# Bias tables moved to GpSimd, an earlier batch load, other drains between GpSimd's sums, and filler products on TensorE

## What is computed

```python
# 1: group norm, 8 heads of 16, two relative-position biases, causal in t
att = einsum('bhqd,bhkd->bhqk', q, k) / sqrt(16) + bias_t + bias_p
x = x + (softmax(where(causal, att, -inf)) @ v) @ Wo
# 2: additive attention on the layer-normed tokens, HID = 16
hidden = tanh(A[:, :, None, :] + B[:, None, :, :])      # 768 x 768 x 16 per batch
t = t + softmax(hidden @ w2 + b2) @ v
# 3: mixture of 8 experts, top 2, capacity 1920, layer norm before
slot = position of the token among those of its expert, over all batches
t = t + sum over 2 experts of weight * (gelu(x w1 + b1) w2 + b2)
```

## Time and profile before

| what | value |
|---|---|
| median of 3 runs | 2385.2 us (2379.06 to 2388.39) |
| the profiled execution | 2384.78 us, of which the trace's span is 2383.0 us |
| mean granted TensorE clock | 0.951 |
| busy share of the span | PE 86%, ACT 71%, DVE 70%, POOL 61% |
| first exponential on ScalarE | 92.63 us |
| first full pass to last full pass | some 122 us a pass |
| pass 14, pass 15, pass 16 start | some 1876, 1977 and 2064 us |
| first expert product | 2124.64 us |

### The profile page before, as it was taken

The page is one execution under the profiler, slowest core; times in us unless marked ns, Lnnn a source line. Parts: engine busy times, 40 slices in busy tenths (PEclk is TensorE's granted clock), DMA queues, the critical chain, the costliest instruction groups (busy, mean ns, idle before and its releaser), DMA issues.

```text
span 2383.0 us, 56242 instructions
## 1 busy us (share of the span) xinstructions
PE 2053.2 (86%) x17665; PEld 1122.5 (47%) x17665; DVE 1675.7 (70%) x4534; ACT 1683.2 (71%) x1933; POOL 1461.3 (61%) x1525
## 2 busy tenths in 40 slices
PE   2889999989998999989998999999999977549986
PEld 1344444444444444444444444444444433338775
DVE  5787787787878787868786878787877665324433
ACT  5238787877887788778787878788878977613332
POOL 3006576656666656565666666666657877627777
PEclk7799999999999999999999999999999988869998
DMA  4546322322222223222323131313131000025553
GB/s 94 89 86 128 95 48 61 55 62 56 61 56 61 56 59 57 58 60 51 66 50 68 42 70 29 81 32 77 32 65 32 12 6 4 7 54 90 84 86 37
DMA packets 157499, 137.99 MB, mean 58 GB/s; under 512 B 24665, under 2 KB 149814, under 8 KB 157104
## 3 DMA queue, kind: packets, MB, share of 16 engines
q1 hardware_dynamic: 119376, 109.87, 22.5%
q0 software_dynamic: 23824, 16.85, 5.2%
q10 hardware_dynamic: 13968, 7.30, 1.2%
HBM read 82.68 MB, written 54.52 MB: 58 GB/s over the span
## 4 chain that ended last, share of the span: by engine, by line
PE 39%; DVE 22%; issue 13%; DVEq 9%; POOL 6%; ACT 4%; POOLq 3%; DMA 2%; SPq 0%; another core or an unknown queue 0%; ACTq 0%
PE logits L978 12%; DVE max_halves L1261 4%; POOL out_dram L583 4%; PE ring L1052 3%; PE av_bank L964 3%; POOLq L802 3%; PE ring L1074 3%; PE ring L1066 3%; PE scores L948 3%; PE scores L951 2%; ACT hidden L902 2%; DVE logit_bias L1447 2%; POOL hidden L803 2%; PE ring L1071 2%; DVEq L1448 2%
## 5 line engine op out<-in xcount | busy, mean ns | idle before, releaser
L803 POOL TENSOR_SCALAR hidden<-b_rep,a_cols 128x768 f32<-128x768 f32 x1152 | 1057.1, 920 | 765.6 <-issue 302.9
L902 ACT ACTIVATE hidden<-hidden 128x2304 f32<-128x2304 f32 x384 | 816.1, 2125 | 16.4 <-POOL hidden L803 16.4
L978 PE MATMUL logits<-hidden,w_shifted 128*32 128x384 f32 x6144 | 591.6, 504 | 65.3 <-ACT hidden L906 30.9
L879 ACT ACTIVATE probs<-scores 128x512 f32<-128x512 f32 (+1 forms) x768 | 391.9, 545 | 325.6 <-PE scores L951 320.9
L1261 DVE TENSOR_REDUCE max_halves<-ring 128x1 f32<-128x384 f32 (+4 forms) x896 | 471.3, 550 | 115.8 <-PE ring L1052 114.2
L906 ACT ACTIVATE hidden<-b_rep,a_cols 128x768 f32<-128x768 f32 x384 | 358.4, 933 | 0.0
L1052 PE MATMUL ring<-k_max,q_max 112*128 112x384 bf16 (+4 forms) x1024 | 296.0, 319 | 34.8 <-DVE max_halves L1261 25.9
L978 PEld LDWEIGHTS logits<-hidden,w_shifted 128*32 128x32 f32 x6144 | 164.0, 110 | 314.9 <-issue 246.7
L948 PE MATMUL scores<-bias_q,onehot_k 112*128 112x512 bf16 (+1 forms) x768 | 276.4, 360 | 4.8 <-ACT probs L879 1.8
L951 PE MATMUL scores<-q_parts,k_parts 98*128 98x256 bf16 (+1 forms) x1536 | 277.3, 262 | 0.0
L814 POOL DMA_INDIRECT expert_rows<-rows,slots x198 | 199.5, 1007 | 64.2 <-issue 32.7
(11 more groups left out here) (262 smaller groups left out, 2585.8 us busy)
## 6 DMA issues: line engine op xcount, KB each, us to landing
qk_parts<-qk_parts_sb SPq DMA_DIRECT2D x16, 1152.0 KB, 4.7
q_parts<-qk_parts SPq DMA_DIRECT2D x192, 96.0 KB, 3.2
k_parts<-qk_parts SPq DMA_DIRECT2D x192, 96.0 KB, 4.3
q_max<-qk_parts SPq DMA_DIRECT2D x96, 96.0 KB
k_max<-qk_parts SPq DMA_DIRECT2D x96, 96.0 KB
expert_rows<-clear_row ACTq DMA_DIRECT2D x9, 792.0 KB, 5.0
x_in<-in_x_dram SPq DMA_DIRECT2D x96, 64.0 KB
x<-in_x_dram SPq DMA_DIRECT2D x96, 64.0 KB
```

Source lines behind the costliest of these rows:

```text
L803: last = g.tensor_scalar(hidden[:, q % SLOTS, o, :], b_rep[:, side], 1.0, a_cols[:, side, a_col(q, o):a_col(q, o) + 1], ALU.mult, ALU.add)
L879: s.activation(probs0[:, d % 3, 2 * pair:2 * pair + 2, 0:n_], scores[:, pair].rearrange("p (j l) -> p j l", j=2)[:, :, 0:n_], ACT.Exp) \
L902: s.activation(hidden[:, t % SLOTS, 0:3, :], hidden[:, t % SLOTS, 0:3, :], ACT.Tanh)
L978: last = mm(logits[32 * g:32 * g + 32, half, 0:HALF], w2_shifted[:, k, :], hidden[:, q % SLOTS, g, HALF * half:HALF * half + HALF], start= ...
```

## The change

- GpSimd, not VectorE, splits the bias table and copies it out to `bias_q[0:64]`, behind its own setup and its first transfer. A new semaphore `bias_made` releases ScalarE's copies (1) and TensorE's first scores (2). Three parts are masked apart and added in two steps.
- SyncE issues `load_x(1)` right after the weight loads, once batch 0 is transposed, and the copies of ScalarE's tables only behind the store of the parts of batch 0. For batch 0 the "k" rest lies in `x2`.
- GpSimd's drains: ahead of each of the three sums at ticks 7 to 18, in all passes; at the other ticks ahead of the third sum only.
- ScalarE: in pass 15 `exp_logits` stands between the two tanh of its tick; at tick 9 of pass 16 a Gelu on one column follows.
- TensorE: `keep_warm(n)` issues n products of 112 x 512 bf16 into the unused `scores` bank, three per tick in pass 15, and 14, 4, 16 and 90 at ticks 3, 7, 8 and 12 of pass 16.

```diff
--- before.py
+++ after.py
@@ -107,6 +107,7 @@
 CLEAR_AT = tuple(range(1, 19, 2))
 CLEARS = 1 + len(CLEAR_AT)
 RING = 3
+WARM_AT = {3: 14, 7: 4, 8: 16, 12: 90}
 PARTS = 4
 
 
@@ -262,7 +263,11 @@
         max_halves = sb("max_halves", [P, H, len(MAX_PARTS)])
         max_parts = sb("max_parts", [4 * TB, 2, 2, P], BF16)
 
-        qk_rest = [xT[:], x_in[:].rearrange("p b c -> p (b c)")]
+        def qk_rest(w, c):
+            if w == 0:
+                return xT[:]
+            return (x_in if positive(c) else x2)[:].rearrange("p b c -> p (b c)")
+
         a_masked = xnT[:, 0:HALF]
 
         q_parts = sb("q_parts", [99, H, L], BF16)
@@ -313,6 +318,7 @@
         setup_pe = sem("setup_pe")
         setup_dve = sem("setup_dve")
         setup_act = sem("setup_act")
+        bias_made = sem("bias_made")
 
 
         sp_passed, pool_passed, act_passed = sem("sp_passed"), sem("pool_passed"), sem("act_passed")
@@ -616,13 +622,18 @@
                 sp.dma_start(b1_col[HID * r:HID * r + HID, :], b1.rearrange("(h o) -> h o", o=1)).then_inc(weights_in, 16)
                 sp.dma_start(w2_col[HID * r:HID * r + HID, :], w2.rearrange("(h o) -> h o", o=1)).then_inc(weights_in, 16)
 
+            sp.wait_ge(ring_filled, 2)
+            load_x(1)
             sp.wait_ge(made, 3)
             sp.dma_start(q_max[48:96, :, :], hot_t.unsqueeze(1).to_broadcast([48, H, L])).then_inc(copies_in, 16)
             sp.dma_start(q_max[96:112, :, :], hot_n.unsqueeze(1).to_broadcast([16, H, L])).then_inc(copies_in, 16)
-            sp.wait_ge(setup_act, 1)
-            sp.dma_start(k_max[48:96, :, :], ct_wide).then_inc(copies_in, 16)
-            sp.dma_start(k_max[96:112, :, :], cn_wide).then_inc(copies_in, 16)
             sp.sem_inc(x2_stored, 16)
+
+            def copy_tables():
+                sp.wait_ge(setup_act, 1)
+                sp.sem_inc(sp_passed, 1)
+                sp.dma_start(k_max[48:96, :, :], ct_wide).then_inc(copies_in, 16)
+                sp.dma_start(k_max[96:112, :, :], cn_wide).then_inc(copies_in, 16)
 
             def store_block(ps, stage, s):
                 b = ps.batch(stage)
@@ -683,7 +694,7 @@
                     if ps.has("pre"):
                         c = ps.batch("pre")
 
-                        if t == 0 and positive(count := c * 2):
+                        if t == 0 and positive(count := c * 2) and positive(c - 1):
                             sp.wait_ge(parts_ready, count)
                             sp.sem_inc(sp_passed, 1)
                             load_x(c)
@@ -693,6 +704,7 @@
                             sp.dma_start(parts_dram[c].rearrange("w p j l -> p w j l"), qk_parts[:, :, :, :]) \
                               .then_inc(parts_stored, 16)
                             if not positive(c):
+                                copy_tables()
                                 load_max(c, 0)
                         if t == SPLIT and positive(c):
                             load_max(c, 0)
@@ -787,6 +799,27 @@
                 signal()
                 pool.wait_ge(made, 5)
                 pool.dma_start(cleared[0], clear_source).then_inc(rows_sent, 16)
+                g.tensor_copy(tn_hi, tn_raw)
+                pool.drain()
+                g.tensor_tensor(tn_rest, tn_raw, tn_hi, ALU.subtract)
+                pool.drain()
+                g.tensor_copy(tn_mid, tn_rest)
+                pool.drain()
+                g.tensor_tensor(tn_lo, tn_rest, tn_mid, ALU.subtract)
+                pool.drain()
+                for r in range(3):
+                    g.tensor_scalar(tn_parts[:, r, :], tn_parts[:, r, :], part_mask[:, r:r + 1], None, ALU.mult)
+                pool.drain()
+                g.tensor_tensor(tn_mid, tn_mid, tn_lo, ALU.add)
+                pool.drain()
+                g.tensor_tensor(tn_all, tn_hi, tn_mid, ALU.add)
+                pool.drain()
+                g.memset(flag[:, 0:1], 0.0).then_inc(bias_made, 1)
+                for h in range(H):
+                    last = g.tensor_copy(bias_q[0:64, h, :].rearrange("p (b n t) -> p b n t", n=16, t=8),
+                                         tn_all[0:64, :].rearrange("p (w h) -> p w h", h=H)[:, :, h][:, ::-1]
+                                         .rearrange("p (b t) -> p b t", t=8).unsqueeze(2).to_broadcast([64, TB, 16, 8]))
+                last.then_inc(bias_made, 1)
 
             def sums(ps, q):
                 b, side = ps.batch("add"), ps.side("add")
@@ -798,7 +831,7 @@
                     pool.wait_ge(logits_added, count)
                     pool.sem_inc(pool_passed, 1)
                 for o in range(3):
-                    if ps.has("max") and (o or TICKS - SEND_FROM < q <= SEND_FROM):
+                    if o == 2 or TICKS - SEND_FROM < q <= SEND_FROM:
                         pool.drain()
                     last = g.tensor_scalar(hidden[:, q % SLOTS, o, :], b_rep[:, side], 1.0,
                                            a_cols[:, side, a_col(q, o):a_col(q, o) + 1], ALU.mult, ALU.add)
@@ -853,7 +886,7 @@
                              cn_raw[:, :, h].unsqueeze(1).unsqueeze(3).to_broadcast([16, TB, 16, 8]), ACT.Copy)
             act.drain()
             s.activation(logit_bias[:, 0:1], ident[:, 0:1], ACT.Copy).then_inc(setup_act, 1)
-            act.wait_ge(setup_dve, 2)
+            act.wait_ge(bias_made, 1)
             for h in range(H):
                 s.activation(bias_q[64:112, h, :].rearrange("p (b n t) -> p b n t", n=16, t=8),
                              tn_all[64:112, :].rearrange("p (w h) -> p w h", h=H)[:, 0:16, h][:, ::-1]
@@ -894,12 +927,14 @@
                         exp_scores(ps.batch(stage), d, 1)
                     if ps.has("end") and t == 1:
                         exp_logits(ps.batch("end"), 5)
-                    if ps.has("add") and t >= 5 and t % 4 == 1:
+                    if ps.has("add") and ps.has("mid") and t >= 5 and t % 4 == 1:
                         exp_logits(ps.batch("add"), t // 4 - 1)
                     if ps.has("add"):
                         b, side = ps.batch("add"), ps.side("add")
                         act.wait_ge(sums_ready, b * 24 + (t + 1))
                         s.activation(hidden[:, t % SLOTS, 0:3, :], hidden[:, t % SLOTS, 0:3, :], ACT.Tanh)
+                        if not ps.has("mid") and t >= 5 and t % 4 == 1:
+                            exp_logits(b, t // 4 - 1)
                         if not positive(b) and t in CLEAR_AT:
                             clear_rows(1 + CLEAR_AT.index(t))
                         col = a_col(t, 3)
@@ -908,6 +943,8 @@
                     if ps.has("end") and t == 9:
                         act.wait_ge(ring_read, ps.number(("end", "gate", 0)) + 1)
                         s.activation(rt[:, 1, :, :], rt[:, 0, :, :], ACT.Exp).then_inc(gate_exp, 1)
+                        if not ps.has("add"):
+                            s.activation(logit_bias[:, 0:1], ident[:, 0:1], ACT.Gelu)
 
             passes(act, body)
             expert_gelu(act)
@@ -924,11 +961,11 @@
                 nc.tensor.transpose(logits[:, 0, P + HID:P + 2 * HID], w1_raw[:, P:2 * P], ident[0:HID, 0:HID])
                 nc.tensor.transpose(logits[:, 0, 192:192 + E], gate_raw, ident[0:E, 0:E])
                 nc.tensor.transpose(logits[:, 0, 256:288], eb1_raw, ident[0:32, 0:32]).then_inc(setup_pe, 1)
-                pe.wait_ge(setup_dve, 4)
+                pe.wait_ge(setup_dve, 2)
                 mm(logits[:, 1, 0:P], wq1_raw, w1T_rep[:, 0].rearrange("p r h -> p (r h)"), start=True, stop=True)
                 mm(logits[:, 1, P:2 * P], wk1_raw, w1T_rep[:, 1].rearrange("p r h -> p (r h)"),
                    start=True, stop=True).then_inc(setup_pe, 1)
-                pe.wait_ge(setup_dve, 5)
+                pe.wait_ge(setup_dve, 3)
 
             pe.wait_ge(made, 1)
 
@@ -936,6 +973,7 @@
                 quad, lo, kb, q0, n_ = STEPS[d]
                 if d == 0 and pair == 0 and not positive(c):
                     pe.wait_ge(made, 4)
+                    pe.wait_ge(bias_made, 2)
                     pe.wait_ge(setup_act, 2)
                 if STEPS[d][1:3] == (0, 0) and pair == 0:
                     pe.wait_ge(score_loaded[quad], c * 192 + 192)
@@ -978,6 +1016,10 @@
                         last = mm(logits[32 * g:32 * g + 32, half, 0:HALF], w2_shifted[:, k, :],
                                   hidden[:, q % SLOTS, g, HALF * half:HALF * half + HALF], start=(k == 0), stop=(k == 3))
                 last.then_inc(logits_added, 1)
+
+            def keep_warm(n):
+                for _ in range(n):
+                    mm(scores[:, 0, :], ones_bf[0:112, :], bias_q[:, 0, 0:512], start=True, stop=True)
 
             def fill(ps, use):
                 stage, name, i = use
@@ -1111,6 +1153,11 @@
                             fill_scores(ps.batch(fill_stage), step, slot)
                         if slot == 2 and q % 4 == 0 and ps.has(stage):
                             add_logits(ps.batch(stage), q)
```

(36 more changed lines are left out.)

## The result

The changed kernel takes 2435.6 us (median of 4 runs, 2431.2 to 2442.3) where the kernel before takes 2382.1 beside it: a ratio of 1.022, 95% interval 1.019 to 1.026. It is slower by 2.2%; the forecast was 2342 us. The profiled execution took 2431.2 us with a span of 2429.4. In the five later sets of runs the kernel before had medians of 2377 to 2386.

The account below looks back on a forecast made before the run. TensorE, busy 86% of the span, was taken as the bound, with gains only where it idles. From 2384.8 us, -20.9 - 12 - 6 - 0 - 1.5 - 2.5 = -42.9 gave 2342 us, range 2318 to 2366.

Parts of the forecast that it names:

- (1) Setup: Start of the kernel: table work leaves VectorE and batch 1 loads earlier, -20.9 us, bounds -21.5 to -12.
- The cover: Setup: GpSimd's and ScalarE's table work ends at least 9 us before it is needed, so it costs nothing.
- Everything behind it ... moves along: Setup: first maxima and first scores hang on VectorE's first copy of batch 1 and come 20.9 us earlier with it.
- (2) Drains in the 14 passes: Passes with a "max" stage: dropping the drain between sums 0 and 1 gives -12 us, bounds -30 to +10.
- GpSimd saves its gap: Ticks 0 to 6 and 19 to 23: GpSimd saves 0.17 us, up to a 0.91 us sum where it waited for a scatter.
- Less 0.8 us in each of the 14 for VectorE: Passes with a "max" stage: VectorE has one window less, priced at 0.8 us per pass, 11 us in all.
- the clock that drops less often: Passes with a "max" stage: reason for rounding the drains' gain of 11 us up to 12.
- the pair of sums locks VectorE out: Rival: with one drain VectorE waits for two sums, 4.4 us per pass, 62 us in 14 passes; 2416 us, chance 0.06.
- (3) First pass without max: Pass from 1876 to 1977: drains give VectorE's operations windows back; half of 12 us, -6, bounds -11 to 0.
- (4) Last pass with sums: GpSimd becomes the bound, its sums taking 84 us, and eats what VectorE and the moved exponential give back: net 0, -6 to +5.
- the case named beside the sum: End of the last pass with sums: if VectorE's unexplained idle of 8.81 us goes, 6.5 us more are won.
- (5) Products and Gelu: Last pass: extra products hold the clock up, -1.5 us at gate products and transposes, -2.5 us at the experts.

Follow-up runs that it names:

- b_setup: Kernel before with the setup part alone (tables on GpSimd, earlier load of batch 1, table copies behind the store): 2400.1 us, ratio 1.009.
- a_old_drains: Changed kernel with GpSimd's drains as before the change, all else kept: 2394.7 us, ratio 1.007 to the kernel before.
- b_new_drains: Kernel before with the new rule for GpSimd's drains alone: 2408.7 us, ratio 1.014.
- b_delay: Kernel before with one more VectorE reduction of 0.92 us per pass ahead of the last x1 normalizations, drains untouched: 2418.9 us, ratio 1.014.
- a_second: Changed kernel with the single drain of ticks 0 to 6 and 19 to 23 ahead of the second sum, not the third: 2374.8 us, ratio 0.998.
- a_sec_fill: Changed kernel with its single drain ahead of the second sum, plus 5 and 4 filler products ahead of x1n and its transposes: 2357.2 us, ratio 0.989.

## Why the prediction was wrong, by its steps

**(1) Setup, -20.9.** At the first mark it gave 22 us, and the first copy came at 32.80 for a forecast of 33.1. GpSimd was later than the upper bound (66.0, not 63), because the drain's 13.22 us behind the transfer, which the earlier loads had slowed, were in no bound, and steps were dearer: the masks 1.56 us each where VectorE took 0.32, the eight copies 1.44 against 0.74. The cover still held. What failed is "Everything behind it ... moves along": b_setup shows the loop giving the gain back and more. The sum had no term for a move that changes where code lies, which is 16 of these some 38 us; the cause of the rest stays open.

**(2) Drains in the 14 passes, -12, bounds -30 to +10.** This is the step that turned the sign. The twelve full passes alone got 76 us longer, 58 of them by this rule (1545 against 1486 in a_old_drains; by their ratios the two kernels are 1.5% or 36 us apart, with some 15 us won behind the full passes set against it). On the kernel before, the rule costs 31 us in these passes (b_new_drains). Two sentences failed. "GpSimd saves its gap": it did, and waited for TensorE instead. "Less 0.8 us in each of the 14 for VectorE": it was about 2.1 us of VectorE's time (24.9 us on the normalizations of x1 alone over twelve passes) at a place where TensorE waits for it, and the clock on top, which made 0.9 us of delay into 2.8 (b_delay). The sum had no term for the clock but a small gain ("the clock that drops less often"); in the twelve passes the time lost to it went from 27 to 75 us.

The price stood in the earlier trace rows: three normalizations took 3.87 us where no drain gives a window. I used that row as a gain for the pass that gets drains, and not as a cost for the passes that lose them. It comes from the same line, L1217, as the 72 normalizations above.

**The rival "the pair of sums locks VectorE out", 2416, chance 0.06,** had the right sign and the right engine, and named 2.2 us per pass as the point where it decides. The full passes grew by 6.3 us each, by 4.8 through the rule when the setup part is in and by 2.6 without it. Its argument against itself failed: "most of those operations fall at ticks 4 to 6 and 17 to 19". The ones that count fall at 19 and 20, behind which TensorE has nothing else to do. And its mechanism was half right: a_second keeps a pair and loses nothing; it is the long window behind the scatter that went.

**(3) First pass without max, -6:** 103.8 to 98.6, and the same in b_new_drains (98.1). The direction is right, the size partly luck. The pieces named in the text (2.8, 2 to 3, about 3) make some 8.5 us and not 12, so half of them is 4. And from run to run this pass takes 99.5 to 104.6 us with the old rule (102 on average) and 95.3 to 101.9 with the new one (98.5).

**(4) Last pass with sums, net 0 (-6 to +5):** from the last mark to the end 406 to 397, and 396 in b_new_drains, 407 in a_old_drains: so about -9 comes with the drains. The forecast of 84 us for the sums was good (85.8, and 83.3 before). VectorE's idle of 8.81 us did go, the case named beside the sum; in its place stands

```profile
2131.30 0.16 DVE L1347 RECIPROCAL row_scale<-row_sum 128x1 f32<-128x1 f32 x1 [3.02 <-PE ring L1116]
```

But that alone isn't the gain. In a_old_drains the idle is 3.02 us as well; there the sums last 90.4 us, and nothing is won. And a_sec_fill, with one drain too, keeps 7.54 us of it and needs 408 us from the mark to the end. Why the idle comes and goes stays open.

**(5) Products and Gelu, -4:** the gate products of pass 16 took 1.50 us in place of 2.73, as forecast. The part on the experts failed: from the first expert's transposes to the end it is 261.7 us before, 260.7 after. The sum took the 90 products (some 21 us) to fill the gap. They took 19.59 and ended 3.19 us before the expert rows came, TensorE stood still again, and the clock was at 0.50 when it went on, so that its first four products took 2.93 us as before, not 1.48. The last row is the window over them:

```profile
2145.97 19.59 PE L1022 MATMUL scores<-bias_q,ones_bf 112*128 112x512 bf16 x90
2168.74 0.90 PE L464 MATMUL av_bank<-ident,xT 128*128 128x128 f32 x3 [3.19 <-DMA xT<-expert_rows]
...
2171.34 2.93 PE L477 MATMUL scores<-probs1T,probs 128*128 128x384 f32 x4
```
```profile
2168.70:2174.00 5.30, 4.43 (x10) 2.52 (x11) 1.11 (x2) 0.58 (x1) 0.00 (x0) 0.50 0.92 240
```

The range ended at 2366, 70 us short. It was built from bounds of each step, and the bound of step 2 was not one: +10 priced VectorE's windows, but not that a pause of TensorE is paid for a second time in clock.

## To carry to other kernels

A wait that one engine spends idle can be another's only free window on a shared path: before removing it, list what the other engine does beside it, and price those instructions by the rows where no window exists. Where TensorE is nearly always busy, look at the granted clock in short stretches, not at its mean: 0.92 us more of waiting cost 2.8 us a pass here. A few dummy products ahead of the wait held the clock. They pay only if no more of them are issued than the pause holds, and they do nothing if they end 3 us before the wait does, as at the experts. And compare a change with a version of the same code position: every second pass of this loop moved by 1.5 to 2.8 us when 25 instructions were put back ahead of it.
